# All heads' keys in both row halves, 64-column tables, and maxima copied by ScalarE for VectorE

## The reference, cut to what matters

```python
q = split_heads(x @ Wq + bq); k = ...; v = ...          # 4 x 16 x 2048 x 16
scores = einsum('bhid,bhjd->bhij', q, k)
rel = einsum('bhid,pd->bhip', q, rel_key)               # 512 relative keys
rel_idx = clip(j - i + p - 1, 0, p - 1)
bias = take_along_axis(rel, rel_idx)                    # bias[i, j] = q[i] . rel_key[rel_idx]
logits = where(j <= i, (scores + bias) * scale, -inf)
out = softmax(logits) @ v ... @ Wo + bo
# then the experts: for each token the two best of 8, three layers of 256 x 256
```

## Time and profile before

| | us |
|---|---|
| median of 3 runs | 3771.6 (3763.04 to 3772.19) |
| the profiled execution | 3769.35, span 3767.3 |
| TensorE busy | 3241.8 (86%) |
| VectorE busy | 2369.6 (63%) |
| ScalarE busy | 1456.2 (39%) |
| GpSimd busy | 1391.9 (37%) |

### The profile page before, as it was taken

How to read it: one execution, slowest core, us unless ns; L and a number is a source line. 1 busy time by engine, 2 the same in 40 slices (tenths; PEclk the granted TensorE clock), 3 DMA queues, 4 the chain that set the end, 5 groups by cost and what they waited for, 6 DMA issues and landing times. The chain is left out here.

```text
span 3767.3 us, 173211 instructions
## 1 busy us (share of the span) xinstructions
PE 3241.8 (86%) x76960; PEld 2785.4 (74%) x76960; DVE 2369.6 (63%) x4756; ACT 1456.2 (39%) x1765; POOL 1391.9 (37%) x1575
## 2 busy tenths in 40 slices
PE   6777999899989999998999999989999999379980
PEld 4456888787888877787888777878878777368770
DVE  8855667676366666744667677356676771465774
ACT  3631333335422333453233344622333446245551
POOL 5764323223354332225533222254332211212656
PEclk8988999999999998999999899999999999699995
DMA  4863001000311100104111000231010000544654
GB/s 128 245 173 87 29 25 39 30 17 30 108 46 41 39 30 16 30 18 121 43 30 39 30 23 24 57 95 43 30 30 16 26 13 12 166 133 144 197 171 133
DMA packets 243388, 255.20 MB, mean 68 GB/s; under 512 B 99496, under 2 KB 186380, under 8 KB 242524
## 3 DMA queue, kind: packets, MB, share of 16 engines
q1 hardware_dynamic: 222204, 202.68, 18.0%
q0 software_dynamic: 20448, 41.45, 3.6%
HBM read 151.36 MB, written 92.59 MB: 65 GB/s over the span
## 5 line engine op out<-in xcount | busy, mean ns | idle before, releaser
L959 DVE TENSOR_TENSOR att_acc<-att_pm,att_acc 128x512 f16<-128x512 f32 x1920 | 1246.3, 686 | 559.3 <-PE att_pm L1066 288.8
L1039 ACT ACTIVATE att_pt<-att_ps 128x1024 f32<-128x1024 f32 x560 | 573.2, 1024 | 1435.9 <-PE att_ps L1069 1435.9
L1066 PE MATMUL att_ps<-att_qx,table_x 68*128 68x64 f16 x8960 | 727.7, 194 | 6.2 <-issue 6.0
L1069 PE MATMUL att_ps<-att_qz,table_z 128*128 128x64 f16 x8960 | 725.0, 194 | 4.8 <-issue 4.8
L1042 ACT ACTIVATE att_pt<-att_ps 128x1024 f32<-128x1024 f32 x528 | 509.3, 1024 | 422.9 <-PE att_ps L1079 413.2
L1069 PEld LDWEIGHTS att_ps<-att_qz,table_z 128*128 128x128 f16 x8960 | 617.6, 99 | 9.3 <-issue 9.0
L1166 PE MATMUL att_po<-att_pt,att_vn 128*32 128x128 f32 x17408 | 619.2, 284 | 3.2 <-issue 2.9
L1066 PEld LDWEIGHTS att_ps<-att_qx,table_x 68*128 68x128 f16 x8960 | 614.9, 99 | 5.6 <-issue 5.0
L149 POOL TENSOR_TENSOR att_qx<-att_qe,mask_i 64x1024 f16<-64x1024 f16 x128 | 239.5, 1888 | 1026.4 <-PE att_po L1166 984.3
L1166 PEld LDWEIGHTS att_po<-att_pt,att_vn 128*32 128x32 f32 x17408 | 461.6, 113 | 59.6 <-issue 13.5
L1062 PE MATMUL att_ps<-att_qs,att_kn 113*128 113x64 f16 x8960 | 452.9, 194 | 36.9 <-DMA att_qs<-s_m 34.4
(11 more groups left out here) (211 smaller groups left out, 4081.8 us busy)
## 6 DMA issues: line engine op xcount, KB each, us to landing
att_qe<-s_q SPq DMA_DIRECT2D x256, 128.0 KB
moe_xs<-s_h SPq DMA_DIRECT2D x78, 256.0 KB
s_y<-moe_y SPq DMA_DIRECT2D x78, 256.0 KB
s_v<-att_vn SPq DMA_DIRECT2D x32, 512.0 KB, 5.3
att_vn<-s_v SPq DMA_DIRECT2D x64, 256.0 KB, 3.3
att_qs<-s_q SPq DMA_DIRECT2D x128, 66.0 KB
att_kn<-s_k SPq DMA_DIRECT2D x128, 64.0 KB, 2.5
att_x<-in_x SPq DMA_DIRECT2D x64, 128.0 KB
```

The source lines that it names most:

```text
L959: dve.tensor_tensor(held, got, held, ALU.max).then_inc(bank_done, 1)
L1039: act.activation(pt[:, k % 2, :, t * 64:t * 64 + 64].rearrange("p h (x c) -> p x h c", x=2), ps[t][:, :, :].rearrange("p x (h c) -> p x h ...
L1066: last = pe.matmul(groups[:, :, g], keep["table_x"][:, y:y + P], qx[0:G * D + G, s, x * (XQ // G) + g], start=False, stop=(g == XQ // G - ...
L1069: last = pe.matmul(groups[:, :, g], keep["table_z"][:, y:y + P], qz[:, s, x * (XQ // G) + g], start=False, stop=(g == XQ // G - 1), skip_g ...
```

## The change

Keys and queries of all 16 heads lie in both row halves, and a half (e) now stands for 64 of the 128 queries instead of eight heads. kn, kx double; qs holds for each half its 64 queries of all heads. near_scores fills two banks at a time, one for each half: 16 heads x 2 key matmuls of 32 columns, then 8 x 2 table matmuls of 64 columns over 64 rows; for exact scores three such products (hi x hi, lo x hi, hi x lo) instead of table_x and table_z. All matmuls of a pair alternate between partitions 0 and 64. The causal mask leaves the tables: in exact scores of the diagonal it is two pairs of 512-column matmuls (later, equal), for maxima an elementwise minimum with bound in a block's first maximum. far_scores has 64-column matmuls in both halves. A near group waits for two free banks. Values are 17 columns a head instead of 32, in scratch too, and po is zeroed once by one matmul.

ScalarE copies the banks r = 1 and r = 3 of a near pair and r = 3 of a far one into 16-bit buffers cp (two), and VectorE takes the maximum from there; such a bank is free when copied. load_groups issues 32 DMAs of 16 rows in pieces of 64 elements, load_queries eight; GpSimd expands a block in two instructions instead of four. The plan's times are other ones.

```diff
-SLOTS, NG = 4, P // G
+SLOTS, HQ, XQ = 4, P // 2, P // 4
+NG = HQ // G
+VN = D + 1
+QS_IN, QE_IN = 8 * 16, 8 * G * 16
...
-        self.kn = a.sb("kn", [P, NB, HH, P], F16)
-        self.vn = a.sb("vn", [P, NB, H, 2 * D])
-        self.qs = a.sb("qs", [P, SLOTS, 2, HH, P], F16)
-        self.qe = a.sb("qe", [P, 2, H, P], F16)
-        self.qz = a.sb("qz", [P, SLOTS, NG, H, G], F16)
-        self.qx = a.sb("qx", [P, SLOTS, NG, H, G], F16)
-        self.which = a.sb("which", [G, H, G], F16)
-        self.made, self.built, self.spread = a.sem("made"), a.sem("built"), a.sem("spread")
+        self.kn = a.sb("kn", [P, NB, H, P], F16)
+        self.vn = a.sb("vn", [P, NB, H, VN])
+        self.qs = a.sb("qs", [P, SLOTS, H, HQ], F16)
+        self.qe = a.sb("qe", [P, 2, 2, H, HQ], F16)
+        self.qx = a.sb("qx", [P, SLOTS, 2, NG, H, G], F16)
...
-    for u in range(2):
+    for half in range(2):
         for r, rows in ((0, 2 * D), (2 * D, D)):
-            sp.dma_start(dst[64 * u + r:64 * u + r + rows].rearrange("r h t -> r (h t)"),
-                         io["s_k"][n, u, 0:rows].rearrange("r h t -> r (h t)")).then_inc(done, 16)
+            sp.dma_start(dst[64 * half + r:64 * half + r + rows].rearrange("r (u h) t -> r u (h t)", u=2),
+                         io["s_k"][n, :, 0:rows].rearrange("u r h t -> r u (h t)")).then_inc(done, 16)
...
-        for r, rows in ((D, 2 * D + 1), (0, D)):
-            sp.dma_start(att.qs[64 * u + r:64 * u + r + rows, s, u].rearrange("r h t -> r (h t)"),
-                         io["s_q"][n, u, 0:rows].rearrange("r h t -> r (h t)")).then_inc(att.qs_in[s], 16)
+    for half in range(2):
+        for u in range(2):
+            for r, rows in ((D, 2 * D), (0, D)):
+                sp.dma_start(att.qs[64 * half + r:64 * half + r + rows, s, u * HH:(u + 1) * HH, :],
+                             io["s_q"][n, u, 0:rows, :, half * HQ:(half + 1) * HQ]).then_inc(att.qs_in[s], 16)
 
 
 def load_groups(sp, io, att, n):
-    for part in range(2):
-        for u in range(2):
-            sp.dma_start(att.qe[64 * part:64 * part + 64, n % 2, u * HH:(u + 1) * HH].rearrange("p h t -> p (h t)"),
-                         io["s_q"][n, u, part * D:(part + 1) * D].rearrange("r h t -> r (h t)")
-                         .partition_broadcast(G)).then_inc(att.qe_in[n % 2], 16)
-
-
-def expand_groups(pool, keep, att, n, quarter):
-
-    s, u = n % SLOTS, quarter % 2
-    rows, dst = (G * D, att.qx) if quarter < 2 else (P, att.qz)
-    heads = slice(u * HH, (u + 1) * HH)
-    return pool.tensor_tensor(dst[0:rows, s, :, heads, :],
-                              att.qe[0:rows, n % 2, heads].rearrange("p h (g i) -> p g h i", i=G),
-                              keep["mask_i"][0:rows, :].unsqueeze(1).unsqueeze(1).broadcast_to([rows, NG, HH, G]),
+    for half in range(2):
+        for part in range(2):
+            for u in range(2):
+                for i in range(G):
+                    row = 64 * half + i * D
+                    sp.dma_start(att.qe[row:row + D, n % 2, part, u * HH:(u + 1) * HH, :],
+                                 io["s_q"][n, u, part * D:(part + 1) * D, :, half * HQ:(half + 1) * HQ]).then_inc(att.qe_in[n % 2], 16)
+
+
+def expand_groups(pool, keep, att, n, part):
+
+    return pool.tensor_tensor(att.qx[:, n % SLOTS, part],
+                              att.qe[:, n % 2, part].rearrange("p h (g i) -> p g h i", i=G),
+                              keep["mask_i"][:, :].unsqueeze(1).unsqueeze(1).broadcast_to([P, NG, H, G]),
...
+                pool.memset(keep["later"][:, :, :], -1.0)
+                pool.memset(keep["equal"][:, :, :], MASK)
+                pool.memset(keep["bound"][:, :], -LOWEST)
...
-    place_time = lambda i, j, part: 1.1 if part == 2 else 1.45 if near(i, j) else 0.3
-    step_time = {"near": 0.47, "far": 0.15, "turn": 0.44, "rows": 0.12, "norm": 0.44, "back": 0.22, "out": 0.43,
+    place_time = lambda i, j, part: 1.1 if part == 2 else 1.1 if near(i, j) else 0.25
+    step_time = {"near": 0.32, "far": 0.13, "turn": 0.44, "rows": 0.12, "norm": 0.44, "back": 0.22, "out": 0.43,
...
+    by_copy = lambda kind, r: kind in ("near", "far") and (r == 3 or r == 1 and kind == "near")
+    copies = [m for steps in plan.values() for m, _, s, _ in steps if by_copy(s[0], s[3] if len(s) > 3 else 0)]
+    copy_of = {m: c for c, m in enumerate(copies)}
...
-            if number >= NBUF:
-                eng.wait_ge(bank_done, number - NBUF + 1)
+            last = number - NBUF
+            if last in copy_of:
+                eng.wait_ge(copied, copy_of[last] + 1)
+            elif last >= 0:
+                eng.wait_ge(bank_done, last + 1)
...
-                    full = pm[number % NBUF]
-                    dve.wait_ge(bank_full, number + 1)
+                    full = pm[number % NBUF][:, :]
+                    if number in copy_of:
+                        dve.wait_ge(copied, copy_of[number] + 1)
+                        full = cp[:, copy_of[number] % 2]
+                    else:
+                        dve.wait_ge(bank_full, number + 1)
...
-                            dve.tensor_scalar(held, got, LOWEST, None, ALU.max).then_inc(bank_done, 1)
+                            dve.scalar_tensor_tensor(out=held, in0=got, scalar=LOWEST,
+                                                     in1=keep["bound"][:, first_query:first_query + XQ].unsqueeze(1).broadcast_to([P, H, XQ]),
+                                                     op0=ALU.max, op1=ALU.min).then_inc(bank_done, 1)
...
+                def bank(number, behind, kind, n, *_):
+                    if number in copy_of:
+                        c = copy_of[number]
+                        act.wait_ge(bank_full, number + 1)
+                        if c >= 2:
+                            act.wait_ge(bank_done, copies[c - 2] + 1)
+                        act.activation(cp[:, c % 2], pm[number % NBUF][:, :], ACT.Copy).then_inc(copied, 1)
+                order(score=score, bank=bank, step=step)
...
+                pe.matmul(po[:, :, :].rearrange("p c t -> p (c t)"), nought[:, :], keep["equal"][:, :, :].rearrange("p h c -> p (h c)"),
+                          start=True, stop=True)
...
+                def near_scores(banks, keys, n, j, t, exact):
+
+
+                    s, last, diagonal = n % SLOTS, [None, None], exact and n % NB == j
+                    groups = [b.rearrange("p (h g i) -> p h g i", h=H, i=G) for b in banks]
+                    for h in range(H):
+                        for e in range(2):
+                            rows = slice(64 * e, 64 * e + KM + exact)
+                            pe.matmul(banks[e][:, h * XQ:(h + 1) * XQ], keys[rows, h, :], qs[rows, s, h, t * XQ:(t + 1) * XQ],
+                                      start=(h == 0), stop=False, skip_group_check=True)
+                    if diagonal:
+                        for e in range(2):
+                            rows = slice(64 * e, 64 * e + 64)
+                            pe.matmul(banks[e], keep["later"][rows, t], keep["equal"][rows].rearrange("p h c -> p (h c)"),
+                                      start=False, stop=False, skip_group_check=True)
+                    products = ((0, 0), (1, 0), (0, 1)) if exact else ((0, 0),)
+                    for g in range(XQ // G):
+                        for table, part in products:
+                            for e in range(2):
+                                rows = slice(64 * e, 64 * e + 64)
+                                y = REL0 + 1 - G - (n % NB - j) * P - (e * HQ + t * XQ + G * g)
+                                last[e] = pe.matmul(groups[e][:, :, g], keep["table"][rows, table, y:y + P],
+                                                    qx[rows, s, part, t * (XQ // G) + g], start=False,
+                                                    stop=(g == XQ // G - 1 and table == 0 and part == exact), skip_group_check=True)
+                    return last
+
+                def far_scores(banks, n, j, t, exact):
...
+                            rows, head = slice(64 * e, 64 * e + KM + exact), HH * t + h
+                            last[e] = pe.matmul(banks[e][:, h * HQ:(h + 1) * HQ], kn[rows, j, head, :], qs[rows, s, head, :],
...
+                    pair = kind in ("near", "far")
+                    if pair and r % 2:
                         return
                     bank_free(pe, number)
+                    if pair:
+                        bank_free(pe, number + 1)
+                        banks = [full[:, :], pm[(number + 1) % NBUF][:, :]]
...
-                        last = pe.matmul(po[32 * (h % 4):32 * (h % 4) + 32, h // 4, :], vn[:, j, h, :], pt[:, k % 2, h, :],
+                        last = pe.matmul(po[32 * (h % 4):32 * (h % 4) + VN, h // 4, :], vn[:, j, h, :], pt[:, k % 2, h, :],
```

More of the change, by code:

```diff
@@ L201, in _ @@
                     seen = slice(G - 1 - i, G - 1 - i + TABW)
[L202 to L210 removed]
+                    for part in range(2):
+                        for u in range(2):
```

(32 more changed lines are left out.)

106 lines of the change are left out of this document (46 added, 60 removed).

## The result

The changed kernel takes 4528.9 us (median of 4 runs, 4520.4 to 4533.5) against 3771.9 on the same chip: 1.200 times before, 95% interval 1.197 to 1.204. The prediction was 3552, its range ended at 3660, and the side was wrong; rival 4, with 4173 at a chance of 8%, was the nearest. The profiled execution has a span of 4524.7 us, 757.4 more than before.

What follows compares the result with a forecast made beforehand. TensorE was taken to bound the kernel, busy 86% of the span. TensorE's path -312, waits +40, projection +30 and head of attention +25 sum to -217 us, from 3769.4 to 3552 us; range 3420 to 3660.

Steps and rivals of the forecast that it cites:

- rival 4: Whole kernel slower than before because TensorE can't be fed, at 45 ns a pair: 4173 us, chance 8%.
- The near pairs, TensorE: Near scores in attention: 4.88 us a block pair falls to 3.58 with row halves side by side, saving 364 us.
- The causal mask: Exact scores of diagonal blocks: two pairs of 512-column matmuls replace spare table rows, +31 us on TensorE.
- far pairs: Far scores in attention: eight pairs of 64 columns instead of four of 128 per group, +21 us on TensorE.
- The value matmuls: Attention: they load 17 columns instead of 32 but stream the same 128, so nothing (0 to -20 us).
- VectorE and ScalarE: Attention: 824 copied maxima banks, VectorE -236 us, ScalarE +483 us, counting only through TensorE's waits: +40 us (-60 to +120).
- The danger of a VectorE maximum beside GpSimd: Attention: two-SBUF-input maxima blocked by GpSimd's SBUF reads, 115 us lost on VectorE, perhaps +10 on the sum.
- table loads: ScalarE in attention: function table reloads at Exp/Copy changes, 1.28 us x 2 x 824 if they came; none assumed.
- SyncE's queue: More, smaller DMA issues: +30 us in the projection, +25 in the head of attention, hidden in steady state.

Runs made afterwards that it cites:

- pace: Kernel of only TensorE matmuls in the attention's shapes, one long stream for each width; 27.8 to 29.7 ns a matmul in six of seven windows.
- near split: Kernel before, with only each 64-column near-table matmul issued as two of 32 columns; 4177.5 us, 1.139 times before.
- reserve: TensorE-only kernel: nine bursts of 2048 32-column matmuls in row halves, each behind 512-column ones; 27.2 to 28.2 ns a matmul over whole bursts.

## Why the prediction was wrong, point by point

**The near pairs, TensorE: the step that failed.** "64 pairs of 32 columns" at 26 ns and the table pairs "at 30 ns as now: 1.92", sum 3.58 us a block pair. Both prices hold in an uninterrupted group (25 and 29 ns a pair). But I priced matmuls and not instructions. A near block pair went from 160 matmuls to 256, from 320 instructions to 512. At the steady 3.7 us for 256 these need 7.4 us, where the reserve holds no more than one such block pair's worth, and the old 320 need 4.6 and took 4.88: the kernel before had almost no room left. Its 30 ns a matmul are the 64 columns' own price (29 in pace, with TensorE busy 99.6%), which by chance lies just above the supply's 28 to 29, so its trace hardly showed the limit (22 us of idle time without a wait). Over 280 block pairs 7.4 - 4.88 is 706 us, and attention grew by 703; that the two agree so well is partly chance, since value matmuls lend some of the time and the other groups pay some of it.

**Rival 4** named the mechanism ("TensorE can't be fed"), with 45 ns a pair and 38 as its point of decision. The sustained pair of four instructions costs 56 to 59 ns in the run of matmuls alone. I gave it 8% because "nothing in the trace runs at this pace for long": true, and the reason to doubt the forecast, since nothing showed that it could. The far groups, my evidence against, are bursts of 16 to 48 instructions, and can live off the reserve.

**The causal mask** (+31) and the **far pairs** (+21). The far groups cost 124 us more: without pauses they run in 358 us, where 0.35 x 1056 = 370 was forecast, but 137 us of pauses follow them against 41 before. The split alone, in the old kernel, cost 38 us. The mask's 256 matmuls take 32.9 us in the trace, start to start, so that term was right.

**The value matmuls** at "nothing". They cost 189 us more: 144 us of pauses against 32, and 37.2 ns each instead of 32.8. With the pauses the granted clock falls, 0.83 in attention instead of 0.96; TensorE spends some 1190 us of attention at the lower level, 1.2 GHz, against 200. In the old kernel with as many instructions in the near groups but without the pauses (near split) it stayed at 0.97. I take that part of the loss for a consequence of the pauses; what it is worth by itself wasn't measured.

**VectorE and ScalarE** (waits +40): TensorE's waits for VectorE in attention proper went from 179 to 231 us. The copies cost 596 ns (forecast 586); the maxima on 16-bit operands 425 ns in the median, 454 on the mean (forecast 400). But only 696 of the 824 copied banks go there. The other 128 belong to a block's first maximum, with bound, which takes 692 ns from the copies and 689 from PSUM: the sum counted a saving on them that wasn't there. The danger of a VectorE maximum beside GpSimd was weighed at a fifth of the maxima and 0.7 us each; it was 94 of 824 at about 0.5 us more. In the changed kernel the copies still gain a little (0.8%); in the old one the standing still costs some 2.5%. No table loads came between Exp and Copy.

**SyncE's queue** (+30, +25): +20.1 and +34.5, 54.6 where 55 was forecast. One row each of SyncE in the projection and in the head:

```profile
127.08 37.90 SPq L144 DMA_DIRECT2D att_qe<-s_q  x59
...
272.04 45.37 SPq L144 DMA_DIRECT2D att_qe<-s_q  x64
```

64 group issues take 45.4 us, 0.7 each, not the 0.5 of the sum; the errors of the two terms, -10 and +9.5, cancel by luck. In steady state it isn't all hidden: the later blocks i = 0 went from 18 to 19 us to 27 to 28, and eight DMAs instead of 32 take about 6 of these back.

The range failed with the mean, as it took in every bound of the columns and none of the instructions.

## What to carry to other kernels

Count TensorE's instructions, loads included, before pricing its matmuls: if a stretch of more than two blocks of 256 asks for one oftener than every 14 to 15 ns, its time is the count times that (by pace and reserve), and there splitting a matmul to run the halves side by side costs time however well the halves overlap. A price read from a short group is a burst price; ask which stretch of the trace, or a kernel of nothing else, sustains it. And before a VectorE operation is moved from PSUM to two 16-bit SBUF operands, look at what GpSimd does in the same microseconds.

## What the runs showed of the hardware that was not expected

- TensorE sustained at most 256 instructions in 3.6 to 3.8 us, at a granted clock of 1.00 as of 0.50, for 32 to 96 columns in row halves and 32 over all rows; a burst of at most 510 ran at 6.2 ns an instruction, later ones of 256 at 6.7.
- A matmul of 32 columns over all rows with its load takes 25 ns start to start, one in row halves 12.5 to 13.4; the Trainium skill (TensorE: Matmul & The Clock Gate, "Wait — 56ns, not 53.3ns?") has about 25 as the floor, which the full rows meet and the row halves beat in bursts.
- A stretch with pauses of 2 us in every 3.7 had a granted clock of 0.50 at 32 columns (reserve and pace), but of 0.98 at 64 columns with as many pauses (pace); the near split, without the pauses, had 0.97.
- A 128x512 maximum on two 16-bit SBUF operands took 425 ns against 687 from PSUM, and up to 5.9 us beside GpSimd's expansions.
